# A two-layer post-norm decoder on one core: the setup's queue order cut finer, and all merges, banks and identity products written anew

## The reference, cut to what matters

```
layer 0:  x = norm(x + attention16(rope(q), rope(k), v) @ w_proj + b)      # 16 heads of 16
          x = norm(x + mLSTM-like mixing of x with ctx, 8 heads of 32, gates from Wi, Wf)
          x = norm(x + W_down . quant(relu(gate(quant x))^2 * up(quant x)))  # ternary weights
layer 1:  x = norm(x + attention16(x, x, x) @ w_proj + b)
          x = norm(x + attention16(x, ctx, ctx) @ w_o + b)
          x = norm(x + relu(x @ W1 + b1) @ W2 + b2)
```

## Time and profile before

| | us |
|---|---|
| median of 3 runs | 1567.4 (1564.08 to 1570.49) |
| time of the profiled execution | 1564.33 |
| its span | 1562.4 |
| PE busy | 1461.7 (94%) |
| DVE busy | 1130.5 (72%) |
| ACT busy | 979.1 (63%) |
| POOL busy | 287.9 (18%) |

### The profile page before, as it was taken

How to read it: one execution, slowest core, us unless ns; L and a number is a source line. 1 busy time by engine, 2 the same in 40 slices (tenths; PEclk the granted TensorE clock), 3 DMA queues, 4 the chain that set the end, 5 groups by cost and what they waited for, 6 DMA issues and landing times.

```text
span 1562.4 us, 30959 instructions
## 1 busy us (share of the span) xinstructions
PE 1461.7 (94%) x12196; PEld 943.8 (60%) x12196; DVE 1130.5 (72%) x2007; ACT 979.1 (63%) x1749; POOL 287.9 (18%) x277
## 2 busy tenths in 40 slices
PE   7889999999999999999999999999899999998998
PEld 5455665566665665556666566555576556564757
DVE  5888989646567897865655889886545889976642
ACT  2477676755657856575365876766546586666572
POOL 6111121022221111111222120101232211111110
PEclk9899999999999999999999999999999999999999
DMA  9351224443332112443332121344423202244310
GB/s 270 119 138 47 68 63 129 119 95 104 91 82 69 49 61 62 138 120 87 101 93 81 22 69 34 100 131 110 116 82 95 62 21 63 62 125 113 109 42 27
DMA packets 128895, 139.46 MB, mean 89 GB/s; under 512 B 11378, under 2 KB 102258, under 8 KB 128754
## 3 DMA queue, kind: packets, MB, share of 16 engines
q1 hardware_dynamic: 128754, 137.50, 32.4%
HBM read 68.91 MB, written 42.99 MB: 72 GB/s over the span
## 4 chain that ended last, share of the span: by engine, by line
PE 51%; DVE 14%; DMA 9%; ACT 8%; issue 3%; SPq 2%; POOL 0%; DVEq 0%; ACTq 0%
PE psum L731 9%; PE psum L962 7%; PE psum L841 7%; PE psum L970 5%; PE psum L724 5%; DMA QK<-heads_dram 5%; PE psum L804 4%; PE psum L823 4%; PE psum L764 3%; DMA heads_dram<-U 3%; ACT PB L1034 3%; DVE nm L1207 3%; PE psum L718 2%; DMA YX<-U 1%; DVE PB L1312 1%
## 5 line engine op out<-in xcount | busy, mean ns | idle before, releaser
L1207 DVE TENSOR_REDUCE nm<-psum 128x4 f16<-128x1024 f32 x384 | 458.3, 1223 | 159.6 <-PE psum L804 158.2
L1034 ACT ACTIVATE PB<-psum 128x1024 f32<-128x1024 f32 x288 | 288.8, 1023 | 85.6 <-PE psum L823 84.5
L841 PE MATMUL psum<-PB,V 128*32 128x256 f32 x2304 | 205.0, 386 | 7.3 <-ACT PB L1034 4.8
L804 PE MATMUL psum<-QK 48*128 48x256 f16 x1536 | 139.2, 275 | 42.2 <-DMA QK<-heads_dram 29.3
L1366 POOL TENSOR_TENSOR YX<-YX 128x512 f32<-128x512 f32 x48 | 60.9, 1269 | 569.7 <-ACT YX L1043 569.6
L1372 POOL TENSOR_TENSOR XO<-XO,row_b 128x512 f32<-128x512 f32 x80 | 101.9, 1283 | 298.5 <-ACT YX L1002 291.7
L823 PE MATMUL psum<-QK 49*128 49x256 f16 x1536 | 139.5, 273 | 11.7 <-ACT PB L1034 3.9
L804 PEld LDWEIGHTS psum<-QK 48*128 48x128 f16 x1536 | 55.7, 94 | 119.7 <-issue 55.2
L962 PE MATMUL psum<-YX,W 128*128 128x256 f32 x512 | 121.4, 387 | 0.2 <-ACT YX L1002 0.2
L841 PEld LDWEIGHTS psum<-PB,V 128*32 128x32 f32 x2304 | 77.7, 109 | 65.2 <-issue 21.7
L970 PE MATMUL psum<-W,PB 128*128 128x256 f32 x512 | 117.1, 382 | 0.0
(11 more groups left out here) (172 smaller groups left out, 2670.4 us busy)
## 6 DMA issues: line engine op xcount, KB each, us to landing
QK<-heads_dram SPq DMA_DIRECT2D x96, 512.0 KB, 4.1
heads_dram<-U SPq DMA_DIRECT2D x288, 128.0 KB, 2.0
YX<-U SPq DMA_DIRECT2D x96, 256.0 KB, 4.0
XO<-in_x SPq DMA_DIRECT2D x16, 256.0 KB, 4.0
YX<-in_ctx SPq DMA_DIRECT2D x16, 256.0 KB, 4.0
out<-XO SPq DMA_DIRECT2D x16, 256.0 KB, 3.2
W<-in_w SPq DMA_DIRECT2D x2, 1024.0 KB, 7.1
heads_dram<-PB SPq DMA_DIRECT2D x4, 256.0 KB, 8.8
```

Of the source, the lines that this page charges most:

```text
L804: ins = pe.matmul(b[:, e * 512 + t * TOK:e * 512 + (t + 1) * TOK], QS[L][r, unit, t * P:(t + 1) * P], KS[L][r, unit, :], start=True, stop= ...
L841: ins = pe.matmul(b[SLOT * j:SLOT * j + SLOT, at:at + TOK], value(L, t, e, u), src, start=(t == 0), stop=(t == TT - 1))
L1034: act.activation(weights_of(L, unit), b[:, 0:1024], ACT.Exp, scale=HD ** -0.5)\
L1207: dve.tensor_reduce(nm[L][:, :, :, unit].rearrange("p t e -> p e t"), b[:, 0:1024].rearrange("p (e t k) -> p e t k", e=2, t=TT), AX.X, ALU ...
```

## The change: what it does

Three things, all in the order and none in what is computed.

1. The setup steps `raws` and `tables` on SP are cut: the constant rows become a step `slots`, the raw weights three steps (unit 2 is w_down, 0 w_gate, 1 w_up), the tables two (the row table, the staged weights).
2. The merges of all five engines (`TURNS`) are new. On SP the setup stands now as `first`, `slots`, row table, staged weights, w_down, w_gate, w_up, all ahead of lane 0's first `qk`. On DVE `sums` moves from ahead of lane 1's first `qk` to behind it, and lane 2's rope from between lane 0's two `qk` steps to behind them; on ACT `permute` moves behind lane 1's v, and lane 1's context copy ahead of lane 0's first `qk`. On PE the first three steps are x of lanes 2, 1, 0 (before 1, 0, 2), and then rope of lanes 0, 0, 1, 2, 1 (before 1, 0, 1, 0 and later 2); lane 3's first rope step comes ahead of lane 0's first `max`. Elsewhere neighbours change places: of PE's 1,777 steps 876 keep their position and 76 move by more than three, of DVE's 966 steps 652 and 8.
3. `PLACES` and `FILL` are new: 1,383 of 1,665 first banks differ, and there are 178 identity products for 145. In the first 21 placements there are 38 for 18, in the next 79 there are 26 for 20, in the rest 114 for 107.

```diff
-        steps = [("first", 0), ("raws", 0), ("tables", 0), ("permute", 0), ("sums", 0), ("scales", 0), ("ternary", 2), ("ternary", 0), ("ternary", 1),
+        steps = [("first", 0), ("slots", 0), ("tables", 0), ("tables", 1), ("raws", 2), ("raws", 0), ("raws", 1), ("permute", 0), ("sums", 0), ("scales", 0), ("ternary", 2), ("ternary", 0), ("ternary", 1),
                  ("weights", 0), ("masks", 0), ("weights", 1), ("weights", 2), ("weights", 3), ("weights", 4)]
...
     "sp": (
-        "4440000001111114042222122333033031124442323300001101100020212200112333301111223220010223031113302000"
+        "4444444000000111111404222212233303301312443224330000011110002012220011233331101122302001222330111323"
...
 FILL = (
-    "9000000000000000009000000000000030500000000000300000000101000010000100000003000200000000000000000000"
+    "9001000000900000009910000000000605000000000000200000000101001010000200000004000300000000000000000000"
...
-                elif name == "raws":
+                elif name == "slots":
                     sp.wait_ge(set_pool, 2)
                     load(slots_set, *[(heads_dram[L][:, :, 3].rearrange("j e r u t -> r (j e) (u t)"), last_rows) for L in range(LANES)])
-                    load(raw_loaded, (raw[2].rearrange("p (k n) -> p k n", k=IT), kt_major(w_down)),
-                         (raw[0].rearrange("p (k n) -> p k n", k=KT), kt_major(w_gate)), (W_1[:, :, :], kt_major(w_up)))
+                elif name == "raws":
+                    load(raw_loaded, ((raw[0].rearrange("p (k n) -> p k n", k=KT), kt_major(w_gate)), (W_1[:, :, :], kt_major(w_up)),
+                                      (raw[2].rearrange("p (k n) -> p k n", k=IT), kt_major(w_down)))[unit])
+                elif name == "tables" and unit == 0:
+                    load(rows_loaded, (row_b[:, :, :], rows.rearrange("(a n) d -> a n d", a=1).to_broadcast([P, 7, DIM])))
                 elif name == "tables":
-                    load(rows_loaded, (row_b[:, :, :], rows.rearrange("(a n) d -> a n d", a=1).to_broadcast([P, 7, DIM])))
                     load(staged_in, (staged[0].rearrange("p (k n) -> p k n", k=KT), kt_major(w_qkv1)[:, :, 0:2 * DIM]),
                          *[(staged[n].rearrange("p (k n) -> p k n", k=KT), kt_major(w)) for n, w in ((1, wq), (2, wk))])
```

More of the change, by code:

```diff
@@ L49 @@
     "down1": "pe dve act",
-    "first": "sp", "raws": "sp", "tables": "sp", "weights": "sp", "masks": "dve", "permute": "act", "sums": "pe dve", "scales": "dve", "ternary": "dve",
+    "first": "sp", "slots": "sp", "raws": "sp", "tables": "sp", "weights": "sp", "masks": "dve", "permute": "act", "sums": "pe dve", "scales": "dve", "ternary": "dve",
 }
@@ L170 @@
[L170 to L174, removed]
@@ new lines @@
+        "2123122101300033030100210223003023030032032220322032030122201132322333303332031310320111233130110321"
+        "12131212125222512331122213222332332232321332331331112333123323262237373333688"),
+    "act": (
+        "2010010021413120302230000030010300110111111111101200221022220221000120001032202101120111020301230333"
+        "1013333013320321013201021213222132123301231330231023320230020000323000232002332100310311301121131111"
+        "3133211221121220312202020220020000322300303223332013323113301011311130310001103301010320255122122322"
+        "1112212212213113231236633322022233300033300220300223000137703303331010013311031031010121188120221002"
+        "2201221021221201120311032032011231330303232313301320213020221312113233102333211132122332102303300001"
+        "0200023001212312303011013310011113103031132311222112220222002200020002230003302233323023331330111031"
+        "1031103100101112331302002201222355221222211211122112211233223036633332033033203220030770000031303103"
+        "3330101003333110111011120120228810002212210202221321033213110332032031322001133310220131020310222131"
+        "3232312312133231212331102123003030002000002032002331001311230111311131103133321122222022112000100200"
+        "0221020030223303223323032003301033013013111003102011155112213322232132222211211211213121016613322032"
+        "3332230303223300230000230033103773031303101031113133188101110002102210001201022312222111220132301102"
+        "1303301333102333201203101320212310221322132132121133202320002300203302032000231032003122131001131031"
+        "1131103131133113130120020000220220220230022202330333232303303322320323013311013011111321112221222552"
+        "212322331231233131132332331232322333337736688"),
@@ new lines @@
+    "dve": (
+        "1010000221140400100033010111114112223344324222222203031313003330010013000110002121001110101122010132"
+        "3210021200002002033211323223322311313213231113012010230322032232202223030010101010333133333311121221"
+        "1211200223232332002220055011530030333133313002611201600116122111122217337722020332203380322283030380"
+        "0131033010133100021201102210101212101032321002102323012013202310010232311131311113122333223300022032"
+        "2322202213131001000000133333133133112221211102023232220222330005015135000300330332323101311160611162"
+        "1217112212773322222003302333082283030383003131000330101021200121102011210021113230002102023231200220"
+        "1031322131333231121111313321020103032222323202232300001001001331333331332112112120102112222020225233"
+        "0005353000301010003333323213136661111211211112212373772220033803338282022230303313010330301101001011"
+        "0101212010112021031230020012210320231201020223111112321313121233323033002033222022323211010030301000"
+        "221333333333111020221211112333322223252223353333331512236377686788"),
@@ new lines @@
+    "0426062146146502640242650206205602356023030643072726042034627062460742062402674062054042460240124062"
+    "6426064214612042506214062647224627406274202473470460246027420746042704264720462702401424260426420740"
+    "2402467420742043064630642604262064302041643646024064702646450624764523742647240730604274620474270462"
+    "7046214542650246076240214026020476042704134174064206736072456576520645604230653463064203624042641624"
+    "6426024604261246260216412643340264061042046702470247462064036730406240230621624616042634625461402460"
@@ L257 @@
[L257 to L258 removed]
+    "0000000000000000000000000000010000001000000000000000000000000100000000000000000000000002000000000000"
+    "0000000000000000000000000010100000000025100000000000000000000000000000000000000000000000000000000003"
+    "0000000020000000000100000030000010000000000000000000000000000000000000000000000000000000000000000000"
@@ L259 @@
+    "00000000000000100000000000000200000100000000000000000000000000000"
 )
```

114 lines of the change are left out of this document (42 added, 72 removed).

## The result

| | before | after |
|---|---|---|
| median, us | 1567.31 (4 runs, 1564.08 to 1570.49) | 1555.24 (4 runs, 1553.46 to 1557.28) |
| profiled execution: time, span, us | 1564.33, 1562.4 | 1553.93, 1551.8 |
| its mean granted clock | 0.991 | 0.997 |

The ratio is 0.9922, with a 95% interval of 0.9893 to 0.9951. The change makes the kernel faster by 0.75%, 12 us in one measurement and 9 to 11 in the other. The forecast was no change, 1567, with a range that ended at 1558.

A forecast was written before the change was run, and what follows sets the result against it. PE was taken as the bound (busy 1461.7 of 1562.4 us), DVE as pacing after the start's hole. DVE +2.7 − 2.9, later fills +0.5, elsewhere 0: +0.3 on median 1567.4, rounded down to 1567; range 1558 to 1576.

The forecast's parts named there:

- Order of SP's setup: SP at the start: all seven setup steps stay ahead of lane 0's parts; staged weights come earlier, last raw later, about 35.1.
- Rival (d): SP's start: raws behind lane 0's stack would take 7.6 us off its path, 1560; chance 0.11 together with another rival.
- Lane 0's chain and the sums: Start: stack lands at 42.4 (+0.8); DVE's sums of the raws end at 45.0, making lane 0's first maximum 2.7 us late.
- Identity products and clock at the start: PE's start: 20 more products cost nothing as DVE is busy; the kept clock gives back 2.9 us.
- cancels, as forecast: Start: DVE +2.7 − 2.9 = −0.2 us at lane 0's last maximum; no change had chance 0.56.
- the old hole: PE's idle stretch from 31.7 to 41.7 us, waiting for lane 0's stack, then clock 0.50 to 48.2.
- the 2.9 of the row: Start: of 3.25 us gained on PE at full clock, only DVE's idle of 2.41 + 0.47 = 2.9 can come back.
- Merges and banks elsewhere: Beyond the start: few steps move far, bank ages distributed as before; effect on 18.7 us of stack waits taken as 0.
- the later fills: PE beyond the start: 13 more identity products cost 0 to 5.9 us, taken as 0.5 since they stand at planned idle.
- rival (b): Whole run: new merges save half the 18.7 us of stack waits, start 1.5 better; −10.8, 1556.6; chance 0.16.
- my own signs of being wrong: First score tile before 41 or after 46; low clock in hole; stack waits over 6 us off; end differing without the start.

The follow-up runs named there:

- raws_behind: rest_new with the three raw weights behind lane 0's stack on SP and their sums later on DVE and PE; 1557.9 us, 0.9943 against the kernel before.
- rest_new: Old setup and start up to PE's step 128, the changed orders, banks and identity products from there on; 1557.7 us, 0.9942 against the kernel before.
- after_again: The changed kernel measured once more, nothing altered; 1558.6 us, 0.9928 against the kernel before.
- start_new: The changed setup, merges, banks and identity products up to PE's step 128, the old ones from there on; 1571.6 us, 1.0034 against the kernel before.
- cold_start: The changed kernel without the 20 identity products that the change adds to the start; 1563.8 us, 0.9959 against the kernel before.
- warm_start: The kernel before with 18 more identity products in the start, nine ahead of lane 1's v and nine ahead of its q; 1568.4 us, 1.0002.
- rest_oldfill: rest_new with the old numbers of identity products from PE's step 128 on; 1566.6 us, 1.0008 against the kernel before.
- old_age_banks: The kernel before with, from PE's step 128 on, each use taking the PSUM banks free the longest; 1642.5 us, 1.0489.
- rest_nofill: rest_new without its 111 identity products from PE's step 128 on; 1578.2 us, 1.0072 against the kernel before.

## Why the prediction was wrong

*Order of SP's setup: right.* First lane 0 part at 31.24 (said 30.7), last of the six issues ending at 34.9 (34.3). Rival (d) gave 7 us for having the raws behind the stack; with the new rest it gave nothing (raws_behind against rest_new).

*Lane 0's chain and the sums: right.* Permutes from 33.73 (33.0), sums from 38.93 to 45.6 (38.3 to 45.0), first maximum on DVE at 45.51 (45.0).

*Identity products and clock at the start: near in the rows, in part luck at the end.* First score tile at 44.56 (44.3), clock 1.00 through. The eighth maximum ends at 60.9 (59 to 60), 1.1 us late, and lane 0's first norm 3.4 late (1.5 in after_again's profile). In front of the new rest the start is worth 0.14% (after_again against rest_new, less than the intervals), so there it cancels, as forecast; in front of the old rest it costs 0.34% (start_new). That it cancels in the kernel forecast is therefore in part luck. The 20 products, whose cost I put at nothing and whose clock I put at 2.9 us, are worth 0.31% there. Without them cold_start stands 0.17% behind rest_new, which is less than the intervals.

The rule that the clock costs half of the throttled time (the Trainium skill, page "TensorE: Matmul & The Clock Gate", section "HAM oscillation — how this bites in real kernels") would have given 6.8 us for the old hole. warm_start, whose profile has no low clock there, is 3.6 to 3.7 us ahead at its first ten norms. But 1.3 us of this lead is there at its first score tile (40.34 for 41.66), whose start lies between 39.8 and 43.1 in the eleven profiles with the old start. From that tile to lane 0's first norm it takes 54.3 us; the kernel before takes 56.6, and ten of the eleven lie between 55.3 and 57.0. So the kept clock gave some 2.3 us in that profile: near the 2.9 of the row, far from the rule's 6.8.

*Merges and banks elsewhere: this is the step that failed.* It read "Bounds: all 18.7 us of the stack waits gone at best; at worst as many again. With no row for a sign I take 0", and 0.5 for the later fills. The rest is worth -0.58% by itself (rest_new), 8 to 9 us. Its direction is that of rival (b), to which I gave a chance of 0.16: stack waits fell by 7.8 us in the changed kernel, by 6.4 in its second profile and by 6.1 in rest_new. That (b)'s price, 1556.6, is 1.4 us from the time measured is luck: it holds 1.5 us from a better start, which was later and not better, and nothing for the clock or for the products, without which the shorter stack waits bring no gain (rest_oldfill). The range ended at 1558, short of even this price. The argument against (b), that shifts by one or two places leave the chain of parts, DRAM and stack as it is, is wrong: at 740 us one lane's parts were issued 20 us earlier (706.73 for 726.98) and its stack 29. Two of my own signs of being wrong came: stack waits more than 6 us from 18.7, and an end that differs although the start doesn't; and PE was busy 1372.6 us from 60 to 1500, 13 more than the 1359 that I gave.

Three things went into the 0 that should not have. I looked at how many steps moved far and how old the banks were, which are counts without a time, and took their smallness for a small effect. I counted the 13 later products as a cost of at most 5.9 us; the 33 products more hold 15 us of PE, but the 111 of rest_new behind step 128 are worth 20 us of time, and the 104 at the old places lose 0.66% against them. And I left no room for waits and clock to act together, as they did at 740 us.

*How the gain divides.* Over 265 executions of these kernels, each taken about its own kernel's mean, the time follows the mean granted clock by 1.3 us for each 0.001 (correlation 0.84). For after_again, 9.4 us below the kernel before in the medians of that group, the clock of 0.9929 against 0.9890 answers to 5.0 and 4.4 are left. For rest_new, 7.7 below at 0.9903 against 0.9896, the clock answers to 0.9 and 6.8 are left. By this the start's products buy clock (cold_start, without them, has a mean of 0.9899), and the new rest buys waits. The division carries a slope found inside each kernel over to differences between kernels; it is worked out and not shown by a run.

*What stays open.* Which of the moves in the rest do it was not found: three pieces of it gave nothing each, and why they don't add up isn't known. Orders and banks could not be taken apart except under a third bank rule, which costs 4 to 5% itself; there the new orders were 1.0% better, so that the new banks are not shown to be needed. The old orders without any products were not run. What is shown is that the gain lies in the rest, and that it needs products placed for its own orders and banks: new orders and banks with the old places gain nothing, and the new places under the old orders lose.

## What to carry to other kernels

When the orders, buffers and fillers of a kernel bound by one in-order engine are all written anew, the sum over the visible stretch (here the start) says little: price the engine's thin waits over the whole run, take the bounds into the range, and do not give the case in which a part of them goes a much smaller chance than that of no change. Counts of moved steps are no price. Neither is one kind of wait: rest_oldfill had the short stack waits without the time. An early lead need not reach the end; warm_start had 3.6 us for 180 us and raws_behind had its first maxima nine us earlier, and neither brought any that could be told. And a profile is one execution: read its lead beside where that execution lies among the others.

## What the runs showed of the hardware

Two executions of one program differ by where the clock falls. In the first profile of the changed kernel the clock was low at 972 and 1409 us, for 6.8 us together; in the second at 971, 1230 and 1312, for 27. One step of that difference can be seen in the rows: PE in the first profile,

```profile
1227.33 0.39 PE L806 MATMUL psum<-QK 48*128 48x256 f16 x4 [1.40 <-DMA QK<-heads_dram]
...
1227.83 0.22 PE L894 MATMUL psum<-M,sel 128*128 128x128 bf16 x1
```

```profile
1232.00:1240.00 8.00, 7.61 (x80) 5.06 (x80) 7.50 (x13) 4.42 (x11) 0.84 (x1) 1.00 0.07 25
```

and in the second:

```profile
1230.52 0.61 PE L806 MATMUL psum<-QK 48*128 48x256 f16 x4 [1.91 <-DMA QK<-heads_dram]
...
1231.36 0.31 PE L894 MATMUL psum<-M,sel 128*128 128x128 bf16 x1
```

```profile
1228.00:1232.00 4.00, 2.09 (x14) 1.16 (x14) 2.23 (x3) 1.05 (x4) 0.00 (x0) 0.76 0.56 122
1232.00:1240.00 8.00, 8.00 (x48) 4.76 (x46) 3.80 (x5) 4.93 (x12) 1.27 (x1) 0.50 0.10 34
```

It is the same wait on the same stack, 1.40 and 1.91 us. Behind the longer one the clock stands at 0.50 (0.31 us for the matmul that took 0.22). The second profile is 2.7 us behind the first at 1221 and 8.9 behind at 1294: half a microsecond more of waiting came with 6 us lost. Why the one execution fell and the other did not is not settled by these two.

The choice of PSUM banks alone can cost 4.9% here (old_age_banks against the kernel before), with the order of every engine and all products unchanged. Over 12 executions rest_new has a mean clock of 0.990, over 7 rest_nofill, without its 111 products, 0.969, and it takes 20 us longer.
